# Dense-tile counts of layers 2 and 3: two loads per group of ten tiles in place of four

## The chip, the cores and the metric

The kernel runs on one core of a Trainium2 chip. The time is device microseconds of one execution; the figure given is the median of several runs. The engines are TensorE (PE), VectorE (DVE), ScalarE (ACT), GpSimd (POOL) and SyncE (SP); DMAs are issued by ScalarE, SyncE and GpSimd and run on 16 DMA engines.

## What is computed

A graph network on 6250 nodes with 128 features and 100000 edges sorted by destination: three layers that average neighbours, a norm, one gated edge layer with edge attributes, and a norm.

```python
def sage_layer(x, src, dst, Wl_i, bl_i, Wr_i):
    msg = x[src]
    agg = segment_sum(msg, dst, 6250)
    cnt = segment_sum(ones, dst, 6250)
    mean = agg / clip(cnt, 1.0)[:, None]
    return mean @ Wl_i + bl_i + x @ Wr_i

h = x
for i in range(3):
    h = sage_layer(h, src, dst, Wl[i], bl[i], Wr[i])
    if i < 2:
        h = relu(h)
x = layernorm(x + h)
z = concatenate([x[dst], x[src], edge_attr], axis=-1)
msg = sigmoid(z @ Wf.T + bf) * softplus(z @ Ws.T + bs)
agg = segment_sum(msg, dst, 6250)
...
```

The change concerns the `segment_sum` of the second and third of the three averaging layers.

## The kernel before

Nodes lie in 49 windows of 128. Edges lie in 784 tiles of 128. Each averaging layer first has y = h @ Wl in DRAM and then sums y over the edges in two ways.

**Dense tiles.** 256 tiles whose 128 edges go to at most 12 neighbouring destinations are summed without a gather. Ten tiles make a group, 26 groups in all. For each group there is a table `counts`, 128 x (49 x 128) bf16: how often each node is the source of an edge to each of the group's rows. Layer 1 makes these tables and stores them in DRAM (`counts_dram`); layers 2 and 3 read them back. There, TensorE multiplies the table with y, window by window: 49 multiplies of 128x385 (y stands as three bf16 parts and a column of ones) that add up in one PSUM bank, `DENSE_BANK`. VectorE then reduces the bank (`reduce_group`), and the next group may start. There is one buffer for the table. It is loaded in four pieces, windows 0 to 12, 13 to 24, 25 to 36 and 37 to 48 (`PIECES`, line 67); a piece is 416 KB (the first) or 384 KB. ScalarE issues the load of a piece of the next group when TensorE has multiplied that piece of this group (`next_piece`, line 1375), and TensorE waits for it and for the y chunks that the piece needs (`multiply_piece`, line 959).

**Gathered tiles.** The other 528 tiles make 132 quads of four. GpSimd gathers the rows of y for each tile with an indirect DMA (`sage_gathers`, line 754, the DMA at line 760) into a ring of twelve quads. The list of indices of a quad comes with a small DMA on SyncE's queue (`sage_quads`, line 565, the DMA at line 575): the first twelve lists are given without a wait, each later one when the items that read the quad twelve places before have been summed. TensorE sums quads by items (`item`, line 941): four matmuls with one-hot matrices that VectorE builds three items ahead (`add_item`, line 2033, which also adds the sum to `acc`). A layer has 182 items in turns of seven; a turn begins with loads of registers on TensorE (`load_turn`, line 921) and on VectorE. Windows that are covered by dense tiles alone have an item too, so the first quads are read only some items into the layer.

**The order.** In the first 17 turns TensorE goes item by item, and behind an item comes a piece: counting items from 0 through a pair of turns, piece p of a group follows the items 0, 1, 2, 3 of each five (lines 991 to 1004). VectorE reduces a group ahead of the adding of the items 4, 9 and the next 0. At a layer's start y comes back from DRAM in seven chunks of seven windows, and VectorE splits each into its three parts (`split_y`, line 2003): two chunks ahead of each of the first adds. In the last nine turns the dense sums come back from DRAM and are added as pairs.

**Layer 3 besides.** ScalarE also reads edge attributes (392 KB a turn) and stores parts of them (eight stores of 196 KB a turn), between its loads of pieces (`attributes`, line 1342; the places stand in `pair_of_turns`, line 1380). VectorE makes those parts (`ea_split`, line 1942).

Four semaphores say that a piece has landed (`s_piece`, line 389); the last two of them are used again for edge attributes later (`ea_given`, line 634).

Of the kernel before, what the change touches and what calls it, by code (L numbers as in the profile page):

```python
# [27 lines left out]
RQ = 12  # L28
# [3 lines left out]
RC = 7  # L32
# [3 lines left out]
NGR = -(-KT // GT)  # L36
# [27 lines left out]
CSLOT = 6  # L64
SLOT_E = P + CELLS
NS_ROWS = 84
PIECES = [(0, 13), (13, 25), (25, 37), (37, 49)]
PAIRS_OF_TURNS = (NGR - 2) // 3
WOVEN = PAIRS_OF_TURNS * 2 + 1
LOOK = 2  # L70
# [33 lines left out]
def build_gnn(nc, x, xT, src, dst, srcT, ea, eaT, w0, bl, blT, w1, we, b1, bn, out):  # L104
# [11 lines left out]
    with ctx:  # L116
# [3 lines left out]
        def sem(name):  # L120
            return ctx.enter_context(nc.semaphore(name))
# [109 lines left out]
        def y_parts(w, n):  # L231

            a, w_ = (yp_pq, w) if w < IN_PQ else (yp_sh, w - IN_PQ)
            return a[:, w_ * YB:(w_ + n) * YB].rearrange("p (u f) -> p u f", f=YB)
# [151 lines left out]
        s_quad = [sem(f"s_quad{q}") for q in range(RQ)]  # L386
        s_ea = [sem(f"s_ea{g}") for g in range(RC)]
        s_load = [sem(f"s_load{q}") for q in range(RC)]
        s_piece = [sem(f"s_piece{p_}") for p_ in range(2)] + s_ea[RC - 2:RC]
        s_idx = (s_load + s_ea)[0:RQ]  # L390
        BELOW = 3 * CW
        assert BELOW * F <= NW * F + UB * 2 * F - RC * QT * 2 * F
# [1 line left out]
        GIVEN = 3 * (QG // RQ) * 16  # L394
# [12 lines left out]

        def tails(p_):

            return (1, 0, 0, 0)[p_]  # L410

        def pairs_added(layer):

# [2 lines left out]
        def pieces_used(layer):  # L416

            return 2 * KP + (layer - 1) * NGR * len(PIECES)

# [42 lines left out]
        def _(sp):  # L462
# [169 lines left out]
            done_regs = [sp.alloc_register(f"sp_d{q}") for q in range(RC)]  # L632

            def ea_given(q):
                return GIVEN if RC + q < RQ else 2 * NGR * 16

            def give_indices(q, at):
                sp.dma_start(idx[:, q * QT:(q + 1) * QT], srcT_sb[:, bass.ds(at, QT)]).then_inc(s_load[q], 16)  # L638
# [167 lines left out]
        def _(pe):  # L806
# [107 lines left out]
            def sage_sums(layer):  # L914
# [6 lines left out]
                def load_turn(it):  # L921
                    for k in range(0, IT, 4):
                        pe.reg_load(t_regs[k:k + 4], q_regs[0:1, bass.ds(it * WIDE + (NEEDED_AT + k), min(4, IT - k))])
                        pe.reg_load(g_regs[k:k + 4], q_regs[0:1, bass.ds(it * WIDE + (PLACES_AT + k), min(4, IT - k))])
                    for i in range(IT):
                        pe.reg_alu(q_needed[i], t_regs[i], 1, ALU.max)
                        if layer:
                            pe.reg_alu(q_needed[i], q_needed[i], layer * QG, ALU.add)
                    return [pe.snap(r, min_val=0, max_val=(RQ - 1) * QT * FA) for r in g_regs]
# [11 lines left out]
                def item(it, i, place):  # L941
                    pe.wait_ge(s["added_items"], it * IT + (layer * NI1 + i + OHS + 1 - sum_back(i)))
                    pe.wait_ge(s["onehots"], it * IT + (layer * (NI1 + OHS - 1) + i + 1))
                    pe.wait_ge(s["landed"], q_needed[i])
                    for u in range(QT):
                        last = te.matmul(ps[:, SUM_BANKS[i], 0:FA], lhsT=oh4[:, OH_SLOTS[i], u, :],  # L946
                                         rhs=shared[:, bass.ds(place + u * FA, FA)], start=u == 0, stop=u == QT - 1)
                    last.then_inc(s["summed"], 1)

                def multiply(it):  # L950
                    pe.wait_ge(s["counts_put"], it * (GT * 2) + (layer * KP + GT) * 2 + 3)
                    pe.wait_ge(s["reduced"], it + (layer * NGR + 1))
                    pe.wait_ge(s["y_split"], NCH)
                    for w in range(NW):
                        last = te.matmul(ps[:, DENSE_BANK, 0:YB - 1], lhsT=counts[:, w, :], rhs=y_parts(w, 1)[:, 0, 0:YB - 1],  # L955
                                         start=w == 0, stop=w == NW - 1)
                    last.then_inc(s["multiplied"], 1)

                def multiply_piece(it, p_):
                    pe.wait_ge(s_piece[p_], it * 16 + ((layer - 1) * NGR + layer * tails(p_) + 1) * 16)  # L960
                    if p_ == 0:
                        pe.wait_ge(s["reduced"], it + (layer * NGR + 1))
                    pe.wait_ge(s["y_split"], layer * NCH + -(-PIECES[p_][1] // CW))
                    for w in range(*PIECES[p_]):
                        last = te.matmul(ps[:, DENSE_BANK, 0:YB - 1], lhsT=counts[:, w, :], rhs=y_parts(w, 1)[:, 0, 0:YB - 1],  # L965
                                         start=w == 0, stop=w == NW - 1)
                    last.then_inc(s["counted"], 1)
# [19 lines left out]
                def counts_before(m, position, counts_at):  # L987
                    for k in range(sum(counts_at[0:position]), sum(counts_at[0:position + 1])):
                        count(m * (3 * GT), k, k % CSLOT)

                if layer:
                    with pe.Fori(0, PAIRS_OF_TURNS) as m:
                        for half_ in range(2):
                            places = load_turn(m * 2 + half_)
                            for i in range(IT):
                                item(m * 2 + half_, i, places[i])
                                group, p_ = divmod(half_ * IT + i, 5)
                                if p_ < len(PIECES):
                                    multiply_piece(m * 3 + group, p_)
                    places = load_turn(WOVEN - 1)  # L1000
                    for i in range(IT):
                        item(WOVEN - 1, i, places[i])
                        for group, p_ in {0: ((0, 0), (0, 1)), 1: ((0, 2), (0, 3)), 3: ((1, 0), (1, 1)), 4: ((1, 2), (1, 3))}.get(i, ()):
                            multiply_piece(NGR - 2 + group, p_)
                else:
                    with pe.Fori(0, PAIRS_OF_TURNS) as m:
                        for half_ in range(2):
                            places = load_turn(m * 2 + half_)
                            for i in range(IT):
                                counts_before(m, half_ * IT + i, COUNTS_AT)  # L1010
                                item(m * 2 + half_, i, places[i])
                                if half_ * IT + i in (4, 9, 13):
                                    multiply(m * 3 + (4, 9, 13).index(half_ * IT + i))
                    places = load_turn(WOVEN - 1)
                    for i in range(IT):
                        counts_before(PAIRS_OF_TURNS, i, COUNTS_LAST)
                        item(WOVEN - 1, i, places[i])
                        if i in (3, 6):
                            multiply(NGR - 2 + (3, 6).index(i))
# [204 lines left out]
        def _(act):  # L1224
# [85 lines left out]
            def sage_counts(layer):  # L1310
# [31 lines left out]
                def attributes(it, half_, step):  # L1342
                    if step == 0:
                        if not isinstance(it, int) or it > 0:
                            store_parts(it - 1, 1 - half_)
                    else:
                        if not isinstance(it, int) or it > 0:
                            parts_stored(it - 1)
                        act.wait_ge(s["ea_in"], it * 16 + 16)
                        alone(act)  # L1350
                        if not isinstance(it, int) or it < EA_TURNS - 1:
                            load_attributes(it + 1, 1 - half_)
# [6 lines left out]
                def load_piece(it, p_):  # L1359
                    a, b = PIECES[p_]  # L1360
                    act.dma_start(counts[:, a:b, :].rearrange("p h r -> p (h r)"), counts_dram[bass.ds(it * P, P), a * P:b * P])\
# [13 lines left out]
                def next_piece(g, p_):  # L1375
                    act.wait_ge(s["counted"], g * len(PIECES) + (pieces_used(layer) + p_ + 1))
                    alone(act)
                    load_piece(g + 1, p_)

                def pair_of_turns(m):  # L1380
                    beside = layer == 2
                    for k in range(3):
                        g = m * 3 + k
                        if beside and k == 0:
                            attributes(m * 2, 0, 0)
                        for p_ in range(len(PIECES)):
                            next_piece(g, p_)
                            if p_ == 0 and (not isinstance(g, int) or g > 0):
                                send(g - 1, (k + 2) % 3)
                            if beside and (k, p_) == (0, 1):  # L1390
                                attributes(m * 2, 0, 1)
                            if beside and (k, p_) == (1, 1):
                                attributes(m * 2 + 1, 1, 0)
                            if beside and (k, p_) == (1, 3):
                                attributes(m * 2 + 1, 1, 1)

                if layer == 0:
# [1068 lines left out]
```

## Time and profile before

| what | us |
|---|---|
| median of 3 runs | 3500.41 (3498.85 to 3501.01) |
| the profiled execution, its own time | 3502.18 |
| its span | 3500.4 |
| TensorE busy in the span | 2665.2 (76%) |
| GpSimd busy in the span | 2333.4 (67%) |
| VectorE busy in the span | 2142.4 (61%) |
| first and last multiply of the dense tables in layers 2 and 3 | 876.3 to 2009.8 |

Layer 2's sums run from about 860 to 1524 us of the span, layer 3's from about 1562 to 2230. A timeline row says when an instruction (or several alike) began, how long they took, on which engine and line, and in brackets how long the engine stood idle ahead of them and what ended that. PEclk is the granted clock of TensorE as a share of full speed.

### The profile page before, as it was taken

The numbers are of one execution on the slowest core, as the hardware profiler recorded it, in microseconds if no ns is written. First come the engines' busy times: TensorE is split into PE (matmuls) and PEld (weight loads), VectorE is DVE, ScalarE is ACT, GpSimd is POOL, SyncE is SP. The second block draws the span as 40 slices with busy tenths as digits, with TensorE's granted clock in tenths as the row PEclk, the third lists the DMA queues.
The fourth block names the chain that finished last, engine by engine and source line by source line (L and its number), as shares of the span: only waits on it lengthen the run. The fifth ranks groups of instructions, "written<-read, shape, count | busy, mean of one in ns | idle before, by whom it ended". The sixth has DMA issues, their size and how long they took to land.

```text
span 3500.4 us, 71571 instructions
## 1 busy us (share of the span) xinstructions
PE 2665.2 (76%) x16221; PEld 2000.1 (57%) x16222; DVE 2142.4 (61%) x4932; ACT 1216.7 (35%) x1668; POOL 2333.4 (67%) x2399
## 2 busy tenths in 40 slices
PE   6578988656787775567887855678888888888884
PEld 5345555556564555555555555556666666666653
DVE  6644554446532234467454454668888888888886
ACT  2422333002000000020000000368888888888865
POOL 3567777575777777746777777357777777767610
PEclk8799999777899997788999977899999999999987
DMA  4354444223565562236887642254444444444411
GB/s 149 104 180 147 145 129 145 76 50 108 160 168 146 139 161 60 53 104 205 250 240 222 192 122 58 78 154 126 128 126 127 127 126 127 124 114 121 114 52 37
DMA packets 345986, 454.45 MB, mean 130 GB/s; under 512 B 135643, under 2 KB 260599, under 8 KB 342311
## 3 DMA queue, kind: packets, MB, share of 16 engines
q0 software_dynamic: 88624, 207.58, 21.9%
q10 hardware_dynamic: 101984, 181.27, 16.2%
q1 hardware_dynamic: 155304, 64.77, 7.1%
q8 instruction: 27, 0.44, 0.0%
q14 instruction: 47, 0.39, 0.0%
HBM read 357.03 MB, written 101.90 MB: 131 GB/s over the span
## 4 chain that ended last, share of the span: by engine, by line
POOL 35%; PE 21%; issue 19%; DVE 10%; DMA 9%; DVEq 3%; SPq 2%; ACT 2%; POOLq 0%; ACTq 0%
POOL shared L760 28%; POOL shared L800 8%; DMA shared<-q_dram,idx 6%; PE ps L955 6%; PE ps L946 4%; PE ps L1151 3%; PE ps L938 2%; SPq L638 1%; DVE work L2326 1%; PE ps L965 1%; DVE work L2010 1%; PE ps L1154 1%; DMA counts_dram<-work 1%; DVE work L2335 1%; ACT work L1481 1%
## 5 line engine op out<-in xcount | busy, mean ns | idle before, releaser
L760 POOL DMA_INDIRECT shared<-y_dram,idx x1584 | 1538.5, 971 | 623.3 <-issue 498.9
L946 PE MATMUL ps<-shared,work 128*128 x4368 | 683.0, 306 | 389.9 <-SPq L578 190.6
L800 POOL DMA_INDIRECT shared<-q_dram,idx x784 | 777.6, 992 | 284.0 <-issue 204.9
L946 PEld LDWEIGHTS ps<-shared,work 128*128 128x128 f32 x4368 | 618.6, 216 | 466.7 <-issue 457.1
L2037 DVE TENSOR_TENSOR acc<-acc,ps 128x129 f32 x546 | 156.3, 286 | 901.8 <-PE ps L946 770.9
L1151 PE MATMUL ps<-pq,work 128*128 x1664 | 498.8, 402 | 149.9 <-issue 89.6
L2326 DVE TENSOR_TENSOR work<-ps,shared 128x256 f32<-128x256 f32 x832 | 294.6, 416 | 177.6 <-PE ps L1154 149.4
L1151 PEld LDWEIGHTS ps<-pq,work 128*128 128x128 f32 x1664 | 257.5, 195 | 244.3 <-issue 173.6
L965 PE MATMUL ps<-pq,work 128*128 128x385 bf16 x1456 | 294.1, 352 | 73.2 <-DVE pq L2007 31.3
L1452 ACT ACTIVATE pq<-ps,blT_sb 128x512 f32<-128x512 f32 (+1 forms) x28 | 16.5, 631 | 887.6 <-PE ps L1050 887.6
L1333 ACT CAST work<-ps 128x600 bf16<-128x600 f32 x260 | 159.6, 661 | 339.6 <-PE ps L938 312.5
L1975 DVE SCALAR_TENSOR_TENSOR work<-ps,w_of,dstT_sb 128x512 f32<-128x512 f32 x370 | 274.9, 744 | 0.8 <-issue 0.8
L1533 ACT ACTIVATE work<-work 128x1024 f32<-128x1024 f32 x208 | 219.8, 1057 | 124.3 <-DVE work L2326 123.1
L2335 DVE SCALAR_TENSOR_TENSOR work<-work,ps 128x1024 f32<-128x1024 f32 x208 | 251.3, 1208 | 1.3 <-ACT ps L1543 1.3
L965 PEld LDWEIGHTS ps<-pq,work 128*128 128x128 bf16 x1456 | 149.1, 104 | 174.4 <-issue 77.7
L1475 ACT ACTIVATE rs<-ve 128x7 f32<-128x7 f32 x21 | 4.4, 210 | 688.3 <-DVE ve L2240 687.4
L1170 PE MATMUL ps<-work 128*128 128x128 f32 x1664 | 242.9, 289 | 0.7 <-DVE work L2347 0.7
L1154 PE MATMUL ps<-we_rows,ea_sb 128*128 128x256 bf16 x832 | 231.0, 278 | 0.0
L1170 PEld LDWEIGHTS ps<-work 128*128 128x128 f32 x1664 | 203.0, 192 | 48.4 <-issue 48.4
L1539 ACT ACTIVATE work<-work 128x1024 f32<-128x1024 f32 x208 | 216.6, 1041 | 0.0
L1543 ACT ACTIVATE ps<-work 128x1024 f32<-128x1024 f32 x208 | 213.9, 1028 | 6.6
L965 PE MATMUL ps<-shared,work 128*128 128x385 bf16 x1092 | 199.7, 330 | 2.3 <-DVE shared L2007 2.3
(363 smaller groups left out, 3627.2 us busy)
## 6 DMA issues: line engine op xcount, KB each, us to landing
work<-counts_dram ACTq DMA_DIRECT2D x156, 384.0 KB
counts_dram<-work ACTq DMA_DIRECT2D x26, 1568.0 KB
shared<-y_dram,idx POOLq DMA_INDIRECT x1584
ea_parts<-work ACTq DMA_DIRECT2D x128, 196.0 KB
ea_sb<-ea_parts SPq DMA_DIRECT2D x196, 128.0 KB
work<-counts_dram ACTq DMA_DIRECT2D x52, 416.0 KB
shared<-q_dram,idx POOLq DMA_INDIRECT x784
y_dram<-work SPq DMA_DIRECT2D x21, 448.0 KB, 3.0
```

Source lines behind the costliest of these rows:

```text
L760: pool.indirect_dma_start(msg[:, u, 0:F], None, y_dram, bass.IndirectOffsetOnAxis(ap=idx[:, u:u + 1], axis=0)).then_inc(s_quad[q], 16)
L800: pool.indirect_dma_start(q_ring[:, u * 2 * F:(u + 1) * 2 * F], None, q_dram, bass.IndirectOffsetOnAxis(ap=idx[:, u:u + 1], axis=0)).then_ ...
L946: last = te.matmul(ps[:, SUM_BANKS[i], 0:FA], lhsT=oh4[:, OH_SLOTS[i], u, :], rhs=shared[:, bass.ds(place + u * FA, FA)], start=u == 0, st ...
L965: last = te.matmul(ps[:, DENSE_BANK, 0:YB - 1], lhsT=counts[:, w, :], rhs=y_parts(w, 1)[:, 0, 0:YB - 1], start=w == 0, stop=w == NW - 1)
L1151: te.matmul(o, lhsT=ohT[:, (slot - 1) % 2, t, :], rhs=pq[:, bass.ds(w_of_pair[t] * (2 * F), 2 * F)], start=True, stop=False)
L1154: last = te.matmul(o, lhsT=ea_sb[:, bass.ds(e_of_pair[t] * P, P)], rhs=we_rows[:, :], start=False, stop=True)
L1170: te.matmul(ps_flat[:, bass.ds(blocks[t] * P + AGG_BANK * 512, P)], lhsT=oh[:, (slot - 3) % GB, t, :], rhs=mm[:, (slot - 3) % 2, t, :], st ...
L1533: sc.activation(log_, pre[:, slot % 2, :, :], ACT.Abs).then_inc(s["absd"], 1)
L1539: sc.activation(log_, log_, ACT.Exp, scale=-1.0).then_inc(s["expd"], 1)
L1975: v.scalar_tensor_tensor(out=oh4[:, slot, :, :], in0=(iota_ps if layer else iota[:, :]).unsqueeze(1).to_broadcast([P, QT, P]), scalar=w_of ...
L2326: last = v.tensor_tensor(pre[:, slot % 2, t, :], ps_pre[:, slot % 2, t, :], q_ring[:, bass.ds(slots[t] * (2 * F), 2 * F)], ALU.add)
L2335: v.scalar_tensor_tensor(out=gates, in0=pre_, scalar=0.0, in1=ps_log, op0=ALU.max, op1=ALU.add)\
```

## The change

`PIECES` becomes two: windows 0 to 24 and 25 to 48 (800 KB and 768 KB). TensorE multiplies the first behind the items 1 and the second behind the items 3 of each five. The load of a half goes out when the whole half has been multiplied, and the second half waits for all seven chunks of y, the first for four. The steps for edge attributes stand behind other pieces, since there are no pieces 2 and 3; two semaphores fall away.

```diff
-PIECES = [(0, 13), (13, 25), (25, 37), (37, 49)]
+PIECES = [(0, 25), (25, 49)]
...
-        s_piece = [sem(f"s_piece{p_}") for p_ in range(2)] + s_ea[RC - 2:RC]
+        s_piece = [sem(f"s_piece{p_}") for p_ in range(2)]
...
-            return (1, 0, 0, 0)[p_]
+            return (1, 0)[p_]
...
-                return GIVEN if RC + q < RQ else 2 * NGR * 16
+                return GIVEN if RC + q < RQ else 0
...
-                                if p_ < len(PIECES):
-                                    multiply_piece(m * 3 + group, p_)
+                                if p_ in (1, 3):
+                                    multiply_piece(m * 3 + group, p_ // 2)
...
-                        for group, p_ in {0: ((0, 0), (0, 1)), 1: ((0, 2), (0, 3)), 3: ((1, 0), (1, 1)), 4: ((1, 2), (1, 3))}.get(i, ()):
+                        for group, p_ in {0: ((0, 0),), 1: ((0, 1),), 3: ((1, 0),), 4: ((1, 1),)}.get(i, ()):
...
                             if beside and (k, p_) == (0, 1):
                                 attributes(m * 2, 0, 1)
+                            if beside and (k, p_) == (1, 0):
+                                attributes(m * 2 + 1, 1, 0)
                             if beside and (k, p_) == (1, 1):
-                                attributes(m * 2 + 1, 1, 0)
-                            if beside and (k, p_) == (1, 3):
                                 attributes(m * 2 + 1, 1, 1)
```

On TensorE, at the start of layer 2 (layer 3 has the same rows): the program before, from the third piece of group 0 to the end of the first turn. Rows of 128x385 are multiplies of the dense tables, with their number; a row of 128x129 stands for an item, whose other matmuls are left out.

```order
L965 MATMUL ps<-pq,work 128x385 x3
L965 MATMUL ps<-shared,work 128x385 x9
...
L946 MATMUL ps<-shared,work 128x129
...
L965 MATMUL ps<-shared,work 128x385 x12
...
L965 MATMUL ps<-pq,work 128x385 x13
...
L965 MATMUL ps<-pq,work 128x385 x12
L923 ISA
```

The same place in the changed program:

```order
L965 MATMUL ps<-pq,work 128x385 x3
L965 MATMUL ps<-shared,work 128x385 x21
...
L946 MATMUL ps<-shared,work 128x129
...
L965 MATMUL ps<-pq,work 128x385 x25
L923 ISA
```

The third and fourth pieces of group 0 (12 and 12, the third ahead of item 3) have become one run of 24 behind item 3; the first and second of group 1 (13 behind item 5, 12 behind item 6) one run of 25 behind item 6. L923 begins the register loads of the second turn.

On ScalarE, at the start of layer 2, the loads of y and of the tables before:

```order
L1318 DMA work<-y_dram 128x7x128 x2
L1361 DMA work<-counts_dram 128x1664
L1361 DMA work<-counts_dram 128x1536 x3
L1318 DMA work<-y_dram 128x7x128 x5
L1361 DMA work<-counts_dram 128x1664
L1361 DMA work<-counts_dram 128x1536 x3
L1361 DMA work<-counts_dram 128x1664
L1340 DMA dense_dram<-work 128x129
```

And in the changed program:

```order
L1318 DMA work<-y_dram 128x7x128 x2
L1361 DMA work<-counts_dram 128x3200
L1361 DMA work<-counts_dram 128x3072
L1318 DMA work<-y_dram 128x7x128 x5
L1361 DMA work<-counts_dram 128x3200
L1361 DMA work<-counts_dram 128x3072
L1361 DMA work<-counts_dram 128x3200
L1340 DMA dense_dram<-work 128x129
```

Each group's four loads have become two of twice the size, at the same places between the reads of y and the store of a dense sum. The rows of VectorE, GpSimd and SyncE are the same in both.

## Rows read from the trace of the kernel before

**Rows 1.** Table of stretches: us, then PE, PEld, DVE, ACT, POOL busy, PEclk, DMA.
```profile
875.00:900.00 25.00, 9.62 (x42) 5.68 (x43) 24.42 (x28) 0.00 (x0) 19.12 (x19) 0.70 0.51 155
...
950.00:975.00 25.00, 23.74 (x164) 16.92 (x162) 9.51 (x21) 0.00 (x0) 18.86 (x20) 1.00 0.71 184
```

**Rows 2.** Timeline of GpSimd, layer 2: start, us, what, idle before it.
```profile
912.62 0.95 POOL L760 DMA_INDIRECT shared<-y_dram,idx  x1 [0.31 <-issue]
920.11 0.94 POOL L760 DMA_INDIRECT shared<-y_dram,idx  x1 [6.55 <-DMA idx<-ea_sb]
...
1518.00 0.94 POOL L760 DMA_INDIRECT shared<-y_dram,idx  x1 [0.30 <-issue]
```

**Rows 3.** Waits of GpSimd from the restart on, layers 2 and 3: total, times, longest.
```profile
POOL shared L760 <- issue: 145.7, 478, 0.3
POOL shared L760 <- DMA idx<-ea_sb: 6.9, 2, 6.5
...
POOL shared L760 <- DMA idx<-ea_sb: 9.3, 4, 8.3
```

**Rows 4.** Timeline of SyncE, layer 2.
```profile
917.67 0.49 SPq L575 DMA_DIRECT2D idx<-ea_sb  x1
```

**Rows 5.** Timeline of TensorE, the start of layer 2.
```profile
876.28 4.34 PE L965 MATMUL ps<-pq,work 128*128 128x385 bf16 x13 [9.99 <-DVE pq L2007]
880.41 1.11 PE L946 MATMUL ps<-shared,work 128*128 x8
888.10 3.41 PE L965 MATMUL ps<-pq,work 128*128 128x385 bf16 x12 [6.58 <-DVE pq L2007]
891.35 1.05 PE L946 MATMUL ps<-shared,work 128*128 x8
899.93 1.12 PE L965 MATMUL ps<-pq,work 128*128 128x385 bf16 x3 [7.53 <-DVE shared L2007]
...
903.75 1.38 PE L946 MATMUL ps<-shared,work 128*128 x8
906.27 2.14 PE L965 MATMUL ps<-shared,work 128*128 128x385 bf16 x12 [1.15 <-DVE shared L2007]
908.25 1.95 PE L946 MATMUL ps<-shared,work 128*128 x16
910.04 2.31 PE L965 MATMUL ps<-pq,work 128*128 128x385 bf16 x13
...
913.07 2.14 PE L965 MATMUL ps<-pq,work 128*128 128x385 bf16 x12
916.41 1.16 PE L946 MATMUL ps<-shared,work 128*128 x8 [1.20 <-issue]
```

**Rows 6.** Timeline of VectorE, layer 2: the last cast of y, a reduction.
```profile
905.04 1.09 DVE L2007 CAST shared<-work 128x896 bf16<-128x896 f32 x1
...
908.53 0.55 DVE L2024 TENSOR_REDUCE work<-ps 128x128 f32<-128x384 f32 x1
```

**Rows 7.** Timeline of GpSimd, layer 3: the restart.
```profile
1622.85 0.94 POOL L760 DMA_INDIRECT shared<-y_dram,idx  x1 [8.34 <-DMA idx<-ea_sb]
```

**Rows 8.** Timeline of SyncE, layer 3.
```profile
1618.10 0.48 SPq L575 DMA_DIRECT2D idx<-ea_sb  x1
```

**Rows 9.** Timeline of TensorE, the start of layer 3.
```profile
1610.53 2.31 PE L965 MATMUL ps<-pq,work 128*128 128x385 bf16 x13 [0.63 <-DMA work<-counts_dram]
...
1616.84 1.16 PE L946 MATMUL ps<-shared,work 128*128 x8 [1.14 <-issue]
```

**Rows 10.** Timeline of ScalarE's DMA issues, the start of layer 3.
```profile
1606.35 0.85 ACTq L1361 DMA_DIRECT2D work<-counts_dram  x2
...
1616.21 4.62 ACTq L1294 DMA_DIRECT2D ea_parts<-work  x8
```

**Rows 11.** What TensorE's multiplies of line 965 waited for: us, times.
```profile
  DVE work L2024: 51.7, 29
...
  DMA work<-counts_dram: 0.6, 1
```

## What the change will do to the time: a prediction

> **What bounds the kernel now.** The change touches layers 2 and 3 alone (numbered 1 and 2 in the code), so I looked there first, in this order: the table of stretches, then GpSimd's timeline, then SyncE's and TensorE's at the one place where GpSimd stands still.
>
> In the stretches TensorE looks like the bound: it is busy 23.74 of 25 us at 950 to 975 [rows 1]. GpSimd shows 18.86 there and looks less busy, but it never stops. Its gathers follow each other every 1.248 us from 920.11 to 1518.00, which is 479 steps in 597.9 us [rows 2], and between each two it waits for nothing but its own issuing: of the 480 gathers after the restart 478 have 0.30 us of "issue" ahead, and the only long wait is the one at the restart itself, in both layers [rows 3]. The last gather ends the layer: the last items wait for it. So each layer's end is the restart plus a fixed stretch, and TensorE's pace in between counts only if it makes GpSimd wait again.
>
> The restart is what matters. GpSimd has room for twelve quads (48 gathers). It fills them, stops at 913.6, and stands 6.55 us until 920.11 [rows 2]; in layer 3 it stands 8.34 us until 1622.85 [rows 7]. It waits for a list of indices, and SyncE gives that list only when the items that read quad 0 are summed. SyncE issues it at 917.67 [rows 4], and the item that ended just before is the one that TensorE began at 916.41 and ended at 917.57 [rows 5]. This is the first item of the second turn, item 7 counting from 0. In layer 3 it is the same item, 1616.84 to 1618.0, and the list goes out at 1618.10 [rows 8, 9]. **Whatever delays item 7 delays the whole layer by as much, and what comes later is hidden behind GpSimd.**
>
> What sets item 7? VectorE splits y into bf16 parts, chunk by chunk, and its last cast starts at 905.04 and lasts 1.09 us [rows 6]. Until then TensorE has little to do and stands three times, 9.99, 6.58 and 7.53 us [rows 5]. From 906.27 on it works without a gap worth naming, so the work between 906.27 and item 7 is the path.
>
> **The change part by part.** *What stands between the last split and item 7.* Before, group 0's pieces 2 and 3 need 6 and 7 split chunks; only piece 3 (12 multiplies) is left at 906.27. Then come items 4 and 5, piece 0 of group 1 (13), item 6, piece 1 (12), the turn's register loads, item 7: 37 multiplies. After, windows 25 to 48 are one piece that needs all 7 chunks. At 906.27 there are 24 multiplies left, then items 4, 5, 6, then 25 multiplies of group 1, then the loads and item 7: 49 multiplies. The 12 that were done at 900 now stand behind the split. A multiply at the high clock steps by 0.165 us (12 from 906.27 to 908.25) [rows 5], so this costs 12 x 0.165 = **1.98 us** in each layer. The split itself does not move: VectorE's adds ahead of it wait for items 1 to 3, and these come earlier or early enough.
>
> *The clock.* Before, TensorE came to 906.27 after 1.15 us of rest, with a granted clock at full. After, piece 0 of group 0 starts at 888.1 (4 chunks split), ends near 894, items 2 and 3 end near 896, and TensorE rests for 10 us. Each of the three rests of 6.6 to 10 us in this stretch was followed by work at the lower of the two levels, 1.2 GHz (the stretch shows a granted clock of 0.70 of full [rows 1]): 13 multiplies took 4.13 us to the next row instead of 2.15, which is 1.98 too much; 12 took 3.25 instead of 1.98, 1.27 too much; 12 took 3.82 and the item behind them 1.38 instead of 1.05, 2.17 too much [rows 5]. The mean is **1.81 us**. It may be 1.27, and at most 24 x 0.165 = 4.0 if all 24 run at the lower level; I take the mean since three rows surround it.
> So in layer 2: 906.27 + 3.96 + 1.81 = 912.0; three items at 0.89 (two take 1.79 from 908.25 [rows 5]) to 914.7; 25 x 0.165 to 918.9; register loads 1.36 as before to 920.2; item 7 to 921.4, against 917.57: 3.8 us late.
>
> The Trainium skill ("TensorE: Matmul & The Clock Gate", Part 1, "What's actually happening") speaks against counting this: it calls the ramp under 1% of a typical span and run-variable, and says not to fit a cold count. By it the two clock terms drop out and the sum is 3.6 us lower. I keep them because the rows show all three rests paid for, and GpSimd passes each microsecond on.
>
> *A wait that goes.* In layer 3 the first piece of group 1 was waited for, 0.63 us at 1610.53 [rows 9], since its load is issued only after the last split (1606.35 [rows 10]). After, that piece is needed near 1614.5 and its load of 800 KB is issued as early. Before, 416 KB behind a load of 392 KB landed within 4.2 us of 1606.35; twice the piece by the same rate lands near 1612. So **-0.63 us** in layer 3.
>
> *The list's own way.* From issue to GpSimd's restart it took 2.44 us in layer 2, and 4.75 in layer 3, where eight stores of ea_parts were going out from 1616.21 on, for 4.62 us [rows 2, 4, 7, 8, 10]. After, the load of the next group's 25 windows (800 KB) goes out as soon as piece 0 of group 1 is done, 2.5 us ahead of item 7. In layer 2 I add **0.5 us** (between 0 and the 2.3 by which layer 3's list is slower; nearer 0, since the load has little left to move by then), in layer 3 **0.1** (between -2.3 and +1.3: a larger load stands there, but a busy one stood there before).
>
> The Trainium skill ("DMA: Bandwidth & Descriptors", "Queues, rings and completion order") has each DMA engine take turns between queues, so a small list on SyncE's queue would not wait for all of a large load on ScalarE's, only share its turns. By that alone the 0.5 would be 0; layer 3's 4.75 us, in the rows, is why I don't take it so.
>
> *What costs nothing, and what hides it.* 104 of the 208 load issues go; ScalarE waits for nobody there but counts. A load of 800 KB has 5 items and the other piece to land in, 5 x 0.89 + 3.96 = 8.4 us, where it had 10.4; the case above took 4.2, and TensorE waited for such a load once in two layers, 0.6 us [rows 11]. If that cover goes, TensorE waits, and GpSimd is reached only when a list comes late: quad 13's list follows item 8, now right behind item 7, and quad 14's follows item 9, about 6 us behind item 7 where GpSimd asks for it after 10. The first piece of a group now comes three items behind the last piece of the group before, not two; the reduction that it waits for (0.55 us and a copy [rows 6]) has one item more to hide in. ScalarE's step that sees off the edge-attribute stores moves from position 1 to 3 of a turn and VectorE asks for it at position 4, behind a reduction and an add; were it late, VectorE would stand about a microsecond in every second turn of layer 3, with one-hots built three items ahead. The eight stores stay at position 6. DVE, SP and GpSimd keep their order; the last woven turn and the tail keep theirs.
>
> **Sum.** Layer 2: 1.98 + 1.81 + 0.5 = 4.3. Layer 3: 1.98 + 1.81 - 0.63 + 0.1 = 3.3. Together 7.6 us: the profiled execution (3502.18) would become 3509.8, and the median shown (3500.41) **3508.0**, which is 0.22% more.
>
> **The rivals.**
> *Faster: TensorE sets the pace.* If the woven stretch ended with TensorE, the reductions count: 29 waits of 51.7 us for them [rows 11], and one more item of cover in each, 29 x 0.89 = 26 us, would give 3475. For it speaks TensorE's 23.74 of 25 us; against it, 480 gathers without a wait. It decides only if GpSimd waits again after the restart. 4%.
> *Hardly slower: no clock paid.* The rest is short enough or falls so that the clock stays up: 2 x 1.98 - 0.63 = 3.3 us, with lists unhindered: 3503.7. The rows speak against it, but three are few, and they come from one execution. 20%.
> *Slower still: the larger loads get in the way.* Layer 3's eight stores (196 KB each) and a load of 800 KB stand ahead of the list, or a piece lands late and GpSimd stops a second time: both lists 2.3 us later, or 24 multiplies at the lower level (+2.2 a layer): 3508 + 4.5 = 3512.5 and up to 3516. 10%.
>
> **How the numbers follow.** My forecast, two terms in each layer, 3505.5 to 3511, has 66%. A measurement of this kernel tells some 0.2% from no change, 7.0 us, and 3507.4 lies inside the forecast: I give 43 of its 66 points to times above. Slower: 43 + 10 = 53%. Same: 23 + 20 = 43%. Faster: 4%. The range runs from 3503 (the multiplies alone, the lists a little quicker) to 3512 (the lists at their upper bound); it leaves out the first rival and most of the third.
>
> **What would show it.** GpSimd's wait before the 49th gather: about 10.8 us in layer 2 (6.55 now) and 11.6 in layer 3 (8.34 now), 480 gathers at 1.248 us behind it in both. On TensorE a row of 24 multiplies after a rest of about 10 us that starts with the last split and lasts 5 to 6.5 us, then three items, then 25 multiplies in 4.1. If that row takes 4 us the clock term is wrong; if the list takes longer than 3 us in layer 2 the list's term is; if GpSimd shows other waits, the pace argument is.

## The result: 0.21% slower, and the profile after

The changed kernel takes 3507.99 us against 3500.27 of the kernel before (medians of 18 runs each), a ratio of 1.0021 with a 95% interval of 1.0013 to 1.0028. A second set of runs gave 3510.87 against 3501.69, 1.0025 (1.0016 to 1.0033). The forecast was 3508.0.

GpSimd's timeline shows it at once. In layer 2 (answers to [rows 2]) it stands 10.84 us where it stood 6.55, in layer 3 ([rows 7]) 13.44 where it stood 8.34. Columns as before: start, us, what, idle ahead of it.

```profile
917.01 0.94 POOL L760 DMA_INDIRECT shared<-y_dram,idx  x1 [0.30 <-issue]
928.79 0.94 POOL L760 DMA_INDIRECT shared<-y_dram,idx  x1 [10.84 <-DMA idx<-ea_sb]
930.04 0.94 POOL L760 DMA_INDIRECT shared<-y_dram,idx  x1 [0.30 <-issue]
...
1621.74 0.94 POOL L760 DMA_INDIRECT shared<-y_dram,idx  x1 [0.30 <-issue]
1636.13 0.94 POOL L760 DMA_INDIRECT shared<-y_dram,idx  x1 [13.44 <-DMA idx<-ea_sb]
```

From the restart to the layer's last gather nothing is added; these are GpSimd's waits from there on, layer 2 and then layer 3 (total, times, longest), which answer to [rows 3]:

```profile
POOL shared L760 <- issue: 145.7, 478, 0.3
POOL shared L760 <- DMA idx<-ea_sb: 11.1, 2, 10.8
...
POOL shared L760 <- issue: 146.0, 479, 0.3
POOL shared L760 <- DMA idx<-ea_sb: 13.4, 1, 13.4
```

So the two restarts hold 4.3 + 5.1 = 9.4 us between them. From a restart to the layer's last gather it is 597.9 and 600.1 us, where it was 597.9 and 601.2, so nothing of the change is seen there. One execution of this program lies up to some 8 us from the median (3492.29 to 3504.71 before the change), by what happens elsewhere too: in the profiles taken here the last gather of layer 1 lies between 813 and 821 us, and the edge layer's sums span 1057 to 1065 us, whatever the kernel. So times below are medians, and profiles are read from the last split of y to the restart.

TensorE at the start of layer 2 (answers to [rows 5]) and of layer 3 ([rows 9]):

```profile
892.50 6.14 PE L965 MATMUL ps<-pq,work 128*128 128x385 bf16 x25 [20.52 <-DVE pq L2007]
898.48 1.95 PE L946 MATMUL ps<-shared,work 128*128 x16
910.67 1.12 PE L965 MATMUL ps<-pq,work 128*128 128x385 bf16 x3 [10.25 <-DVE shared L2007]
911.59 4.52 PE L965 MATMUL ps<-shared,work 128*128 128x385 bf16 x21
915.95 2.97 PE L946 MATMUL ps<-shared,work 128*128 x24
918.75 4.29 PE L965 MATMUL ps<-pq,work 128*128 128x385 bf16 x25
923.83 2.05 PE L946 MATMUL ps<-shared,work 128*128 x16 [0.79 <-issue]
...
1614.15 1.12 PE L965 MATMUL ps<-pq,work 128*128 128x385 bf16 x3 [10.41 <-DVE shared L2007]
1615.07 6.02 PE L965 MATMUL ps<-shared,work 128*128 128x385 bf16 x21
1620.93 2.97 PE L946 MATMUL ps<-shared,work 128*128 x24
1623.73 4.29 PE L965 MATMUL ps<-pq,work 128*128 128x385 bf16 x25
1628.81 2.05 PE L946 MATMUL ps<-shared,work 128*128 x16 [0.79 <-DVE work L1975]
```

The reader is to see: a rest of 10.25 and 10.41 us; behind it 24 multiplies in 5.28 us (910.67 to 915.95) and 6.78 us (1614.15 to 1620.93) where the high clock's 0.165 us each would make 3.96; three items; 25 multiplies at the high clock; the register loads; item 7. A stretch over the rest and the first of these runs shows a clock between the two levels, 0.58 of full, so that part of it was at the lower one (a table of stretches; PEclk is the third column from the end):

```profile
905.00:915.00 10.00, 4.33 (x19) 2.26 (x20) 6.25 (x8) 0.00 (x0) 7.56 (x9) 0.58 0.20 52
```

And the list of indices ([rows 4, 8]), with the load that ScalarE issues ahead of it, in layer 2 and in layer 3 ([rows 10]):

```profile
923.14 0.35 ACTq L1361 DMA_DIRECT2D work<-counts_dram  x1
...
925.08 0.49 SPq L575 DMA_DIRECT2D idx<-ea_sb  x1
...
1628.13 0.35 ACTq L1361 DMA_DIRECT2D work<-counts_dram  x1
...
1629.00 5.21 ACTq L1294 DMA_DIRECT2D ea_parts<-work  x8
...
1630.06 0.49 SPq L575 DMA_DIRECT2D idx<-ea_sb  x1
```

The list leaves at 925.08 and GpSimd starts at 928.79: 3.71 us, where it was 2.44. In layer 3 it is 6.07, where it was 4.75.

### The profile page after: what moved, and what is told of

It reads as the page before. It is cut to its first block, busy times and chain, and to the rows that moved or that the text cites. A ratio compares the mean times of both kernels' runs of the same rounds, so it can differ in the third digit from the quotient of the medians.

```text
span 3509.3 us, 71047 instructions
## 1 busy us (share of the span) xinstructions
PE 2672.0 (76%) x16221; PEld 2003.2 (57%) x16222; DVE 2139.3 (61%) x4932; ACT 1216.8 (35%) x1668; POOL 2331.7 (66%) x2399
## 3 DMA queue, kind: packets, MB, share of 16 engines
q10 hardware_dynamic: 87008, 181.26, 15.4%
## 4 chain that ended last, share of the span: by engine, by line
POOL 36%; PE 21%; issue 19%; DVE 11%; DMA 7%; DVEq 3%; ACT 2%; SPq 1%; POOLq 0%; ACTq 0%
POOL shared L760 28%; POOL shared L800 7%; PE ps L955 6%; PE ps L1151 4%; DMA shared<-q_dram,idx 4%; PE ps L946 4%; PE ps L938 2%; DVE work L2326 1%; PE ps L1170 1%; PE ps L1154 1%; DVE work L2010 1%; DVE work L2335 1%; SPq L638 1%; DMA counts_dram<-work 1%; DVEq L1938 1%
## 5 line engine op out<-in xcount | busy, mean ns | idle before, releaser
L965 PE MATMUL ps<-pq,work 128*128 128x385 bf16 x1456 | 284.4, 350 | 77.3 <-DVE pq L2007 38.9
L1533 ACT ACTIVATE work<-work 128x1024 f32<-128x1024 f32 x208 | 219.9, 1057 | 125.9 <-DVE work L2326 125.9
```

Source lines behind the costliest of these rows:

```text
L1533: sc.activation(log_, pre[:, slot % 2, :, :], ACT.Abs).then_inc(s["absd"], 1)
```

## Experiments

The theory: item 7 sets GpSimd's restart; the 12 multiplies moved behind the last split, the clock behind a longer rest and a slower list make it late. Rivals: the larger loads themselves cost the time; TensorE's pace sets the end. The two columns on the list are read from the timelines of one profile each: how long behind the end of the last cast of y the list leaves, and how long it takes from its issue to GpSimd's restart. Then come the change of the median against the kernel before in the same set, and the ratio, which is worked out apart from the medians; the two differ by up to some 2 us (43 matmuls: 6.9 by the medians, 4.6 by 1.0013), so a step of 2 us between two rows decides nothing by itself.

| kernel | layer 2: leaves, takes | layer 3: leaves, takes | median, us | ratio (95%) |
|---|---|---|---|---|
| before (two profiles) | 11.5, 2.4 / 11.5, 2.4 | 12.3, 4.8 / 12.3, 5.7 | 3500.27 | |
| the change (two profiles) | 14.6, 3.7 / 15.4, 3.8 | 16.1, 6.1 / 15.9, 6.2 | +7.7, +9.2 | 1.0021, 1.0025 |
| two loads, four runs | 11.4, 3.5 | 13.6, 5.7 | +3.5 | 1.0007 (0.9998 to 1.0015) |
| four loads, two runs | 14.7, 2.8 | 16.0, 5.9 | +5.7 | 1.0014 (1.0006 to 1.0023) |
| change, wait by chunk | 11.8, 3.9 | 13.2, 6.3 | +2.8 | 1.0011 (1.0002 to 1.0020) |
| change, 26 matmuls in the rest | 13.9, 5.3 | 15.1, 5.8 | +4.7 | 1.0012 (1.0004 to 1.0021) |
| change, 43 matmuls in the rest | 12.5, 6.1 | 12.5, 7.3 | +6.9 | 1.0013 (1.0004 to 1.0021) |
| change, load held back | 15.6, 2.5 | 15.8, 2.4 | +5.6 | 1.0015 (1.0006 to 1.0024) |
| before, items first | 9.7, 2.5 | 8.7, 4.3 | -2.3 | 0.9988 (0.9978 to 0.9997) |
| change, items first | 12.4, 2.7 | 14.0, 2.4 | -0.5 | 1.0002 (0.9994 to 1.0011) |
| before, short path | 6.7, 2.8 | 7.9, 4.9 | -8.0 | 0.9979 (0.9967 to 0.9990) |
| change, short path | 7.0, 3.1 | 7.8, 3.0 | -8.3 | 0.9979 (0.9970 to 0.9988) |

The four list figures of a row added up (31.0 and 31.9 before, 40.4 and 41.3 in the change) follow the medians to within some 2.5 us. Two rows don't: 26 matmuls (8.7 above before, and 4.7 by the median) and the kernel before with items first (6.3 below, and 2.3 by the median). One profile is one execution.

### The change in halves

Loads in two, multiplies in four runs at their old places:

```diff
+RUNS = [(0, 13), (13, 25), (25, 37), (37, 49)]
...
-                    pe.wait_ge(s_piece[p_], ...)
+                    pe.wait_ge(s_piece[p_ // 2], ...)
...
-                    for w in range(*PIECES[p_]):
+                    for w in range(*RUNS[p_]):
```

> Loads as in the change (two of 800 and 768 KB a group), multiplies as before (four runs behind the items 0 to 3 of each five). Theory (12 more multiplies behind the last split make item 7 late): item 7 ends 11.3 us after the last split in layer 2 and about 12 in layer 3, as before; only the list of indices stays slower behind the larger load (3.7 and 6.1 us in the profile of the change, 2.4 and 4.8 before), so the time is that of before plus 0 to 4 us, 2.6 as the likeliest. Rival (the larger loads are what costs): before plus 6 to 9 us, as the change.

Loads in four, multiplies in two runs at the new places:

```diff
-                                if p_ < len(PIECES):
-                                    multiply_piece(m * 3 + group, p_)
+                                if p_ in (1, 3):
+                                    multiply_piece(m * 3 + group, p_ - 1)
...
+                    for k in (p_, p_ + 1):
+                        pe.wait_ge(s_piece[k], ...)
```

> The other half: four loads a group as before, multiplies in two runs as in the change. Theory: GpSimd's waits at the restart are 9.5 to 11 us (layer 2) and 11 to 13.5 (layer 3), the time is before plus 5 to 8 us. Rival (the larger loads cost): waits as before, 6.6 and 8.3 us, and the time within 2 us of before.

With the loads alone item 7's list leaves as early as before in layer 2 (11.4 us) and is itself a microsecond slower there (3.5 for 2.4). In layer 3 it leaves 1.3 later and takes 5.7, which one of the two profiles of before shows too. The 1.3 has a cause of its own: TensorE now waits 2.03 us for the first half of group 1's table, where it waited 0.63 for the smaller piece [rows 9]:

```profile
1613.59 2.31 PE L966 MATMUL ps<-pq,work 128*128 128x385 bf16 x13 [2.03 <-DMA work<-counts_dram]
```

Together +3.5 us, with an interval that just takes in no change. With the runs alone it leaves as late as in the change: +5.7. These are GpSimd's waits with the runs alone, layer 2 and layer 3; they are almost the change's:

```profile
POOL shared L760 <- DMA idx<-ea_sb: 10.4, 2, 10.1
...
POOL shared L760 <- DMA idx<-ea_sb: 13.8, 3, 13.1
```

So the place of the multiplies is the larger part. The size of the loads is the smaller one, by the list in layer 2 and by TensorE's wait for a load in layer 3; in the change itself that wait is gone, since the table is needed later there.

### What holds the 24 multiplies up

The change, with the wait for y taken chunk by chunk:

```diff
-                    pe.wait_ge(s["y_split"], layer * NCH + -(-PIECES[p_][1] // CW))
                     for w in range(*PIECES[p_]):
+                        if w == PIECES[p_][0] or w % CW == 0:
+                            pe.wait_ge(s["y_split"], layer * NCH + w // CW + 1)
```

> The change, but a run of multiplies waits for y chunk by chunk and not for all that the run needs. Theory: behind the last split 7 multiplies are left instead of 24, 17 x 0.165 = 2.8 us fewer in each layer, the clock still low in part: before plus 0 to 4 us. Rival (TensorE's path to item 7 does not set the restart): no difference to the change, before plus 7.7 us.

The list leaves 11.8 and 13.2 us behind the split (14.6 and 16.1 in the change), +2.8 us: as expected. The 17 multiplies go where TensorE rests.

Filling the rest, to see the clock alone (matmuls on constants, into a bank that nothing reads):

```diff
+                                if first and half_ == 0 and i == 3:
+                                    for _ in range(WARM):
+                                        te.matmul(ps[:, 4, 0:P], lhsT=ident[:, :], rhs=ones[:, :], start=True, stop=True)
```

> The change with 26 matmuls on constants, into a free PSUM bank, in TensorE's rest ahead of group 0's second half (first pair of turns of layers 2 and 3 written out). Theory with a clock term: the run of 24 takes 4.0 us instead of 5.3 and 6.8, GpSimd's waits fall by 1.3 and 2.8 us, the time is before plus 3 to 5.5 us. Rival (the clock does not reach the end): as the change, before plus 7.7 us.

The time met the expectation, and the reason did not. The 26 matmuls took 5.97 us and left 4.4 us of rest in layer 2 and 4.8 in layer 3, and the 24 multiplies were still in part at the lower clock: 5.4 us at a granted clock of 0.73, and 6.6 at 0.58. So the run says nothing on what the clock costs. With 43:

> The change with 43 matmuls on constants in the rest ahead of group 0's second half (26 left 4.4 us of it, and the 24 multiplies still took 5.4 and 6.6 us). Theory with a clock term: the 24 multiplies take 4.0 to 4.3 us, item 7's list goes out about 13.3 us behind the last split in both layers (14.6 and 16.1 in the change), the time is the change's minus 3 to 5 us. Rival: the 24 take as long as in the change.

Now the rest is 0.61 us and the 24 take 3.96 (908.11 to 912.07); these are TensorE in layer 2, then the load, the list and GpSimd's restart there:

```profile
908.11 0.66 PE L966 MATMUL ps<-pq,work 128*128 128x385 bf16 x3 [0.61 <-DVE shared L2015]
908.60 3.63 PE L966 MATMUL ps<-shared,work 128*128 128x385 bf16 x21
912.07 2.84 PE L947 MATMUL ps<-shared,work 128*128 x24
...
919.14 0.35 ACTq L1369 DMA_DIRECT2D work<-counts_dram  x1
...
920.42 0.49 SPq L576 DMA_DIRECT2D idx<-ea_sb  x1
...
926.56 0.94 POOL L761 DMA_INDIRECT shared<-y_dram,idx  x1 [11.16 <-DMA idx<-ea_sb]
...
908.00:912.00 4.00, 3.89 (x24) 2.36 (x25) 0.82 (x2) 0.00 (x0) 2.87 (x4) 1.00 0.19 49
```

The last row is a stretch over the 24 multiplies: a granted clock of 1.00. In layer 3 they take 3.96 as well. The clock term is shown: the list leaves 2.1 to 2.9 us sooner in layer 2 and 3.5 sooner in layer 3 than in the two profiles of the change. Some 0.6 us of that is not the clock's: the idle time ahead of item 7 is gone as well. The time fell by 2.3 us by the medians (3508.6 against 3510.87 of the change in the same set) and by 4.2 by the ratios (1.0013 against 1.0025); 3 to 5 were expected, and neither figure can be told from that. In the profile the list now takes 6.1 and 7.3 us, so that in layer 2 the gain is given back whole.

### What the list waits for

The trace's record of DMA packets tells when each moved, in us of the span:

```
place                    load: first packet, last begins   list: issued, first packet   restart
before, layer 2              916.30        918.18           917.67     918.81            920.11
change, layer 2              924.12        926.97           925.08     926.96            928.79
26 matmuls, layer 2          916.87        919.81           917.21     919.78            922.48
43 matmuls, layer 2          920.12        923.07           920.42     923.07            926.56
```

Before, the list's first packet moves 1.14 us behind its issue. In the other three it moves when the last packets of the 800 KB load begin, to within 0.03 us, however early the list was issued. The list is on another queue (SyncE's) and still waits for the load. So the restart hangs on the load as well as on item 7.

The list's way has a second part. In all 14 profiles and both layers GpSimd restarts 0.77 to 0.79 us behind the last of the 16 shares in which a list lands. In the change these land close together (layer 2: the 15th at 928.00, the last at 928.01). With 43 matmuls one share comes alone and late: the 15th at 924.13 and the last at 925.78 in layer 2, 1630.34 and 1632.02 in layer 3. That is 1.65 and 1.68 us, where this list is slower than the change's by 2.4 and 1.2 in all. So most of what the filled rest gave back is not the load's doing. In both layers a packet of 16 KB on the queue of instructions moves just then (923.29 to 924.20, and 1629.20 to 1630.14), and the two profiles of the change show none there; this program has its first pair of turns written out and is longer. The trace does not name the DMA engine of a packet, so this cause is likely and not shown.

Held back, the load can't delay the list:

```diff
+                            if isinstance(g, int) and (g, p_) == (1, 0):
+                                act.wait_ge(s["summed"], layer * NI1 + 10)
                             next_piece(g, p_)
```

> The change, but ScalarE issues the load of group 2's first half (and what stands behind it in its queue, in layer 3 the eight stores of edge attributes) only when item 9 is summed, behind the list that restarts GpSimd. Theory (the load under way slows the list): the list takes 2.4 to 2.7 us in both layers instead of 3.7 and 6.1, item 7 ends where it does in the change, and the time is the change's minus 4 to 5 us, before plus 3. Rival (the list is slow for another reason): no difference to the change.

The list takes 2.45 us in layer 2 (920.48 to 922.93) and 2.42 in layer 3 (1626.83 to 1629.25), as expected of the mechanism. The time fell by some 2 to 4 us (+5.6 against +7.7 and +9.2 in the other sets) where 4 to 5 were expected: the load is now late itself. TensorE waits for it in layer 3, and GpSimd, in layer 2 shown here, waits a second time (13.3 in all, 10.7 the first):

```profile
922.93 0.94 POOL L760 DMA_INDIRECT shared<-y_dram,idx  x1 [10.66 <-DMA idx<-ea_sb]
...
1637.99 7.10 PE L965 MATMUL ps<-pq,work 128*128 128x385 bf16 x25 [3.48 <-DMA work<-counts_dram]
...
POOL shared L760 <- DMA idx<-ea_sb: 13.3, 2, 10.7
```

### Does a microsecond at item 7 pass on?

Group 1's multiplies moved behind the items 8 and 9, in the first pair of turns, on either kernel (the lines shown are of the kernel before):

```diff
+                                if first and at in (5, 6, 7, 8, 9):
+                                    for k in {8: (0, 1), 9: (2, 3)}.get(at, ()):
+                                        multiply_piece(1, k)
```

> The program before, but in the first pair of turns of layers 2 and 3 (written out) group 1's four pieces stand behind the items 8 and 9 (two each) and no longer behind the items 5 to 8. Theory (item 7 sets the restart, and each microsecond passes on): 25 multiplies, 4.1 us, leave the path in each layer; item 7's list goes out about 7.4 us behind the last split (11.5 and 12.3 before) and takes 2.4 us where no load is under way; GpSimd waits 2 to 3 us instead of 6.6 and 8.3. The time is before minus 8 to 11 us. Rival (GpSimd's restart is not what the end hangs on, or another wait takes its place): less than half of that, minus 4 us or nothing.

> The same on the change: group 1's two runs stand behind the items 8 and 9. Theory: item 7's list goes out 10.5 to 12 us behind the last split (14.6 and 16.1 in the change), takes 2.4 us, and the time is the change's minus 10 to 13 us, before minus 2 to 5. Rival as for the other: the change's minus 5 or less.

Both fell short: -2.3 us where 8 to 11 were expected, and 8 to 10 below the change of the other sets where 10 to 13 were. On the kernel before, the list leaves 9.7 and 8.7 us behind the split and not 7.4. TensorE shows why, in layer 2:

```profile
910.24 2.84 PE L946 MATMUL ps<-shared,work 128*128 x24
915.65 3.54 PE L946 MATMUL ps<-shared,work 128*128 x16 [2.57 <-issue]
...
915.65:917.20 1.55, 1.55 (x7) 1.55 (x8) 0.00 (x0) 0.00 (x0) 0.00 (x0) 0.50 0.22 53
```

The register loads of the second turn now show 2.57 us of idle time; behind 12 they showed 1.20 [rows 5] and behind 25, in the change, 0.79. The multiplies had hidden them. The clock fell in the gap (granted 0.50 in the last row, a stretch behind it): 16 matmuls took 3.54 us, not 1.95. A gap of this length does not cost that each time: in layer 2 of the change with items first it was 2.45 us, and 16 matmuls took 2.05 at a granted clock of 1.00. In layer 3 a later list is late too, by 1.64 us, behind a first wait of 4.3.

With the three costs taken out together (wait by chunk, group 1 behind items 8 and 9, half of the second turn's registers loaded ahead of the last split):

```diff
+                                if first and at == 3:
+                                    next_places = load_half(1, 0)
+                                if first and at == 10:
+                                    places = places + load_half(1, 4)
```

> The program before with three edits in the first pair of turns: multiplies wait for y chunk by chunk (7 left behind the last split), group 1's pieces stand behind the items 8 and 9, and the first half of the second turn's registers is loaded ahead of the last split. Theory: item 7's list goes out 5 to 7.5 us behind the last split (11.5 and 12.3 before), GpSimd's wait falls to 1 to 3 us, and the time is before minus 7 to 12 us. Rival (a second wait of GpSimd gives it back, as in part with the items first): before minus 2 to 5 us.

> The same three edits on the change. Theory (the order of the multiplies ahead of item 7 is all that made the change slower): item 7's list goes out 5 to 7.5 us behind the last split, and the time is within 3 us of the same edits on the program before, so before minus 4 to 12 us. Rival (two loads cost something of their own): slower than the other by 5 us or more.

Both are 8 us faster than the kernel before, and equal to each other within the some 3 us that these medians can tell: 3493.68 and 3493.44. In the change's version GpSimd, with its twelve quads filled, stands 2.60 us; TensorE goes from 7 multiplies straight through five items:

```profile
912.40 2.43 PE L975 MATMUL ps<-shared,work 128*128 128x385 bf16 x7 [3.95 <-DVE shared L2029]
914.63 5.48 PE L955 MATMUL ps<-shared,work 128*128 x40
...
922.39 0.94 POOL L760 DMA_INDIRECT shared<-y_dram,idx  x1 [2.60 <-DMA idx<-ea_sb]
...
POOL shared L760 <- DMA idx<-ea_sb: 8.0, 4, 3.0
```

The last row is GpSimd's waits in layer 3: the restart itself is 2.1 us of the 8.0, and two later lists hold it for 5.6. On the kernel before the later waits of layer 3 come to 5.6 us as well. So the rival expected here, a second wait that gives time back, is in part true.

This version beats the kernel before by 0.21% (interval 0.12 to 0.30%), and the change by more; with it two loads cost no more than four that these runs could tell.

### The kernels once more

> The program before once more, for a second profile. If what differs between the profiles outside layers 2 and 3 (layer 1, and the edge layer's 1061.6 us from first to last sum against 1058.3 in the change) is scatter, this one may lie at either value; if it is the change's doing, it shows 1061 to 1062 again.

> The change once more, beside these on one chip: before plus 6 to 9 us, GpSimd's waits near 10.8 and 13.4 us, the 24 multiplies 5 to 7 us.

The kernel before showed 1057.05 us for the edge layer's sums this time, 1061.56 the first: scatter, and no doing of the change. The change's waits were 11.7 and 13.5 us, its 24 multiplies 6.1 and 6.7 us.

## Why the prediction was right, and what was mis-sized

**The place and the way held.** GpSimd's restart was named as what counts, item 7 as what sets it; 480 gathers follow without another wait in both layers, at 1.248 us in layer 2 and 1.253 in layer 3. Halving the change, and the short path on both kernels, confirm it from two sides. "By as much" holds for a later item 7; an earlier one let later lists hold GpSimd, 5.6 us in layer 3 of the short path.

**The 12 multiplies** (1.98 us a layer): confirmed; 24 stand behind the split, and taking 17 of them away brought the list forward by 2.8 and 2.9 us.

**The clock** (1.81 us a layer, between 1.27 and 4.0): measured 1.32 and 2.82, in the second profile 2.12 and 2.71 (the run of 24 less 3.96). The mean is 2.2, within the bounds. The Trainium skill's advice ("TensorE: Matmul & The Clock Gate", Part 1, "What's actually happening") not to fit a cold count would have dropped it. Its figure of under 1% is borne out (4.1 and 4.8 us of some 3508), and so is its remark that the count varies between runs (1.32 against 2.12 in one place). But here these microseconds stood on the path: with the rest filled the list left sooner by all of them.

**Item 7** came 3.0 and 3.8 us later behind the split in the first profile, 3.8 and 3.2 were forecast. The register loads hid better behind 25 multiplies than behind 12 (0.79 us seen against 1.20), which the sum left alone.

**The wait for the first piece of group 1** (-0.63): gone, as forecast. The list of what the multiplies of line 965 waited for has no load in it any more.

**The list** (0.5 and 0.1 us) is the step that was mis-sized: 1.3 us in both layers by the first profiles; in layer 3 0.9 between the means of two profiles each. I took the load to be nearly over when the list comes; it is not (its packets move from 924.12 to 927.22, the list is issued at 925.08), and the list waits for all of it. The prediction read the Trainium skill's page ("DMA: Bandwidth & Descriptors", "Queues, rings and completion order") as if turns by packet made a list share the engines with a load. The page says that an engine drains a whole packet of about 9 to 17 descriptors before it switches; a load of 128 rows on 16 engines is 8 rows each, so by that figure a load is one turn, which is an estimate. The packets above agree with it that far: the list's first began with the load's last. The order behind the load does not come out of turns between queues: ScalarE's small store of a dense sum, issued behind the load on the same queue, landed ahead of the list too (the late shares with 43 matmuls, layer 2: load 925.38, store 925.57, list 925.78).

**The sum** was 7.6 us; the two restarts give 9.4 in the first profiles and the medians 7.7 and 9.2. That the first median is so close to the forecast is partly luck: the list was too small by 2.0 us in the sum (first profiles), and a median of this kernel is uncertain by some 3 us, as the interval of the ratio shows.

**The rivals.** TensorE's pace is refuted: its waits for the reduction fell, from 51.7 us in 29 to 32.3 in 12 ([rows 11]; the row of after is below), as that rival had it, and the time did not follow: those 19 us less of waiting bought nothing. The unpaid clock is refuted in all four runs of 24. The third had the right mechanism (a list behind a load) but not the size: no second wait came in the change. It came when the load was held back.

```profile
  DVE work L2024: 32.3, 12
```

What stays open: what holds the one late share of the list with 43 matmuls in the rest (the 16 KB of instructions are the likely cause), and in what order a DMA engine takes what several queues give it.

## What to carry to other kernels

Look for the engine that runs without a gap and ask what starts it; a microsecond lost there counts in full, and one gained counts until another wait takes its place, while 19 us fewer of waits elsewhere count for nothing. Merging small steps into fewer large ones makes the first of them wait for the last of what they need: give the merged step its waits piece by piece, or move what it delays ahead of it. A tiny transfer that an engine waits for should not be issued right behind a large one, even on another queue.

## What had not been expected of the hardware

A 2 KB list on SyncE's queue waits for an 800 KB load that ScalarE issued up to 1.9 us earlier: its first packet moved 1.14 us behind its issue where no load was under way (load held back, layer 2: 920.48 to 921.62), and up to 2.65 us (920.42 to 923.07) with the load. The lists land in 16 shares, and GpSimd starts 0.77 to 0.79 us behind the last: one share of a list came 1.65 us behind the other 15 (925.78 against 924.13). TensorE's loads of a turn's registers show 2.57 us of idle time when no multiplies are queued ahead of them, and 0.79 to 1.20 when there are. Behind a rest of 4.4 us the 24 multiplies ran at the lower level for a part (granted clock 0.73), behind one of 0.61 us at the high level throughout (1.00); behind the change's rests of some 10 us the lower level cost 1.3 to 2.8 us.
